# Broadcasting B by transposes of a repeated column in a Mamba kernel, with a new order of the front work

## The reference, cut to what matters

```
xi, z = split(x @ in_proj.T)
xc    = silu(causal_conv4(xi) + conv_b)
dt, B, C = split(xc @ x_proj.T)                    # 8, 16, 16 columns
delta = softplus(dt @ dt_w.T + dt_b)
h[t]  = exp(delta[t] * A) * h[t-1] + delta[t] * xc[t] * B[t]    # per channel and state
y[t]  = sum over the states of h[t] * C[t]
out_d = ((y + xc * D) * silu(z)) @ out_proj.T
```

## Time and profile before

| | us |
|---|---|
| median of 3 runs | 3480.59 |
| lowest, highest | 3477.56, 3481.06 |
| profiled execution | 3478.78 |
| its span, first to last instruction | 3477.0 |
| PE busy | 2952.8 (85%) |
| DVE busy | 3042.4 (88%) |
| ACT busy | 3106.2 (89%) |
| POOL busy | 2824.1 (81%) |
| mean granted clock of PE | 0.981 of 2.4 GHz |

### The profile page before, as it was taken

How to read it: one execution, slowest core, us unless ns; L and a number is a source line. 1 busy time by engine, 2 the same in 40 slices (tenths; PEclk the granted TensorE clock), 3 DMA queues, 4 the chain that set the end, 5 groups by cost and what they waited for, 6 DMA issues and landing times.

```text
span 3477.0 us, 53162 instructions
## 1 busy us (share of the span) xinstructions
PE 2952.8 (85%) x18432; PEld 2224.8 (64%) x18432; DVE 3042.4 (88%) x2456; ACT 3106.2 (89%) x5825; POOL 2824.1 (81%) x1701
## 2 busy tenths in 40 slices
PE   5888888888888888888888888888888888888885
PEld 3666666666666666666666666666666666666664
DVE  3889889889889888898898898899898988888986
ACT  4989999999989999999999998999999999999984
POOL 2788888888888888788788888888887888888886
PEclk9999999999999999999999999999999999999998
DMA  2222222222222222222222222222222222222221
GB/s 72 89 72 92 86 86 85 81 83 91 86 86 85 78 91 86 81 88 83 82 86 86 86 91 73 91 85 86 87 89 74 91 86 85 85 81 83 87 81 48
DMA packets 102319, 290.59 MB, mean 84 GB/s; under 512 B 11387, under 2 KB 36262, under 8 KB 102054
## 3 DMA queue, kind: packets, MB, share of 16 engines
q1 hardware_dynamic: 102054, 287.19, 25.4%
HBM read 276.91 MB, written 10.24 MB: 83 GB/s over the span
## 4 chain that ended last, share of the span: by engine, by line
ACT 33%; PE 31%; DVE 20%; issue 14%; POOL 1%; DVEq 0%; SPq 0%; DMA 0%; ACTq 0%; POOLq 0%
ACT da L697 13%; DVE hc L941 10%; PE g_ps L329 8%; DVE g_ps L928 8%; ACT w L643 7%; PE y_ps L329 5%; ACT L684 5%; PE m_ps L362 3%; PE m_ps L413 3%; PE m_ps L371 3%; PE m_ps L329 3%; PE m_ps L429 2%; PE m_ps L391 2%; DVE stats L914 2%; ACT s L667 1%
## 5 line engine op out<-in xcount | busy, mean ns | idle before, releaser
L834 POOL TENSOR_TENSOR hc<-hc,c_all 128x1000 f32<-128x1000 f32 x1024 | 2350.3, 2313 | 522.3 <-DVE hc L941 508.4
L941 DVE TENSOR_TENSOR_SCAN hc<-da,g_ps 128x1012 f32<-128x1012 f32 x1024 | 2274.6, 2253 | 91.4 <-ACT da L697 18.9
L697 ACT ACTIVATE da<-delta,a_neg 128x498 f32<-128x498 f32 x2048 | 1332.9, 700 | 9.0 <-DVE hc L941 7.3
L329 PEld LDWEIGHTS y_ps<-ident,hc 128*125 128x125 f32 x8192 | 1027.7, 190 | 238.8 <-issue 164.3
L329 PE MATMUL y_ps<-ident,hc 128*125 128x128 f32 x8192 | 1081.7, 275 | 2.2 <-POOL hc L834 2.2
L643 ACT ACTIVATE w<-ut,bt 125x256 f32<-125x256 f32 x2048 | 892.8, 497 | 2.9 <-ACT ut L630 0.4
L329 PE MATMUL g_ps<-ident,w 125*128 125x125 f32 x4096 | 547.3, 277 | 370.7 <-DVE hc L941 280.5
L329 PEld LDWEIGHTS g_ps<-ident,w 125*128 125x128 f32 x4096 | 443.9, 142 | 427.1 <-DVE hc L941 326.1
L928 DVE TENSOR_TENSOR g_ps<-u,g_ps 128x1000 f32<-128x1000 f32 x512 | 608.2, 1188 | 80.6 <-PE g_ps L455 80.3
L362 PE MATMUL m_ps<-zt,convw 128*128 128x500 f32 x1024 | 475.6, 587 | 0.7 <-ACT zt L573 0.7
L362 PEld LDWEIGHTS m_ps<-zt,convw 128*128 128x128 f32 x1024 | 190.5, 191 | 148.7 <-issue 121.9
(11 more groups left out here) (62 smaller groups left out, 2314.5 us busy)
## 6 DMA issues: line engine op xcount, KB each, us to landing
c_all<-c_rows SPq DMA_DIRECT2D x512, 500.0 KB, 3.6
xin<-x_t SPq DMA_DIRECT2D x32, 375.0 KB, 3.5
out<-out_sb SPq DMA_DIRECT2D x32, 250.0 KB
c_rows<-dbl SPq DMA_DIRECT2D x64, 31.2 KB, 1.6
c_all<-f_conv_w SPq DMA_DIRECT2D x1, 512.0 KB
c_all<-b_conv_w SPq DMA_DIRECT2D x1, 512.0 KB
hc<-f_in_w SPq DMA_DIRECT2D x1, 128.0 KB
inw<-f_in_w SPq DMA_DIRECT2D x1, 128.0 KB
```

What stands on the lines that cost most here:

```text
L329: return pe.matmul(dst, src, ident[0:rows, 0:rows], start=first, stop=last, is_transpose=True, skip_group_check=True)
L697: op = act.activation(states(da[n % RING])[j].rearrange("p (s t) -> p s t", s=SC)[:, :, 1:T], steps, ACT.Exp, scale=a_neg[:, p % 2, db, 2 ...
L834: pool.tensor_tensor(hc, hc, c_all[:, pair % CRING], ALU.mult).then_inc(hc_ready, 1)
L941: dve.tensor_tensor_scan(h[n % HRING][:, 0:UC], da[n % RING][:], g_ps[n % 2][:, 0:UC], 0.0, ALU.mult, ALU.add).then_inc(scanned, 1)
```

## The change

- B is taken to all partitions by transposes: for r in 0, 1, 3, 5 `fill_g` transposes `bt`'s column for the state, repeated 128 times as the stationary operand, in eight pieces of 125 tokens, in place of two bf16 matmuls. `parts`, `pick`, `minus`, the `split` jobs and copies, and the two inputs for them are gone.
- The front's order is x projection (5), dt (7), softplus (8), `bt` (8), y (9 and 10), u (10 and 11), transposed u (12 and 13). `turn` and the first half of the tail (`out_proj`, ACT's copy) go to step 13; the second half stays at 14. The gated products stand two units behind their y: before units 11 and 12.
- ACT's products for r = 6 and 7 are spread anew.
- `make_w` of POOL is rewritten too, but `W_POOL` is empty, so it isn't called.

```diff
-CONV, GATES, XPROJ, BT, SPLIT1, Y0, SPLIT2, Y1, DT, U0, U1, UT0, UT1 = 0, 4, 5, 6, 6, 6, 7, 8, 9, 11, 12, 13, 14
-TURN, TAIL0, TAIL1, TOKENS = 10, 11, 14, 15
+CONV, GATES, XPROJ, DT, SOFTPLUS, BT, Y0, Y1, U0, U1, UT0, UT1 = 0, 4, 5, 7, 8, 8, 9, 10, 10, 11, 12, 13
+TURN, TAIL0, TAIL1, TOKENS = 13, 13, 14, 15
...
-W_ACT = {2: [(-2, 4), (-1, 4)], 4: [(0, 2), (1, 2), (2, 2), (3, 2)], 6: [(6, 3), (7, 3), (8, 2)], 7: [(10, 2), (11, 3), (12, 3)]}
+W_ACT = {2: [(-2, 4), (-1, 4)], 4: [(0, 2), (1, 2), (2, 2), (3, 2)], 6: [(6, 3), (7, 3), (9, 2)], 7: [(9, 2), (10, 2), (11, 2), (12, 2)]}
...
-    ends = [("y", m - 2, 0), ("y", m - 2, 1), ("dt", m, 0)] if m > 1 else [("dt", m, 0)]
-    return ([("conv", m, 0), ("conv", m, 1), ("gate", m, 0), ("gate", m, 1), ("xproj", m, 0), ("bt", m, 0),
-             ("split", m, 1), ends[0], ("split", m, 2), *ends[1:], ("dt", m, 1)],
-            [("ut", m, 0), ("ut", m, 1)])
+    ends = [("y", m - 2, 0), ("y", m - 2, 1)] if m > 1 else []
+    return ([("conv", m, 0), ("conv", m, 1), ("gate", m, 0), ("gate", m, 1), ("xproj", m, 0),
+             ("dt", m, 0), ("dt", m, 1), ("bt", m, 0)] + ends, [("ut", m, 0), ("ut", m, 1)])
...
-                    src = w[w_index(p, r) % WRING]
-                    for e in range(2):
-                        for j in range(NT):
-                            at = e * BANK + j * TP
-                            mm = turned(g[:, at:at + TP], src[:, e, j, db * 128:(db + 1) * 128], TP)
-                    mm.then_inc(b_filled, 1)
-                else:
-                    if k <= 1:
-                        wait_drained(pe, "split", p, 2)
-                    pe.matmul(g[:, 0:TC], pick[:, 2 * r, :], parts[p % 2][:], start=True, stop=True)
-                    pe.matmul(g[:, BANK:UC], pick[:, 2 * r + 1, :], parts[p % 2][:],
-                              start=True, stop=True).then_inc(b_filled, 1)
+                elif k <= 1:
+                    wait_drained(pe, "bt", p, 0)
+                for e in range(2):
+                    for j in range(NT):
+                        if r in TURNED:
+                            rows = w[w_index(p, r) % WRING][:, e, j, db * 128:(db + 1) * 128]
+                        else:
+                            rows = bt[p % 2][:, j, 2 * r + e:2 * r + e + 1].broadcast_to([TP, 128])
+                        at = e * BANK + j * TP
+                        mm = turned(g[:, at:at + TP], rows, TP)
+                mm.then_inc(b_filled, 1)
...
                 m = bank("xproj", p, 0)
-                act.activation(dbl[:], m[0:XR, 0:TC], ACT.Copy)
-                act.activation(parts[p % 2][:], m[0:K2, 0:TC],
-                               ACT.Copy).then_inc(drained[bank_of("xproj", p, 0)], 1)
+                act.activation(dbl[:], m[0:XR, 0:TC], ACT.Copy).then_inc(drained[bank_of("xproj", p, 0)], 1)
...
-                        if k == DT:
+                        if k == SOFTPLUS:
                             load_set(SOFTPLUS_SET)
                             softplus(m + 1, 0)
                             softplus(m + 1, 1)
                             load_set(EXP_SET)
+                        if k == BT:
+                            bt_copy(m + 1)
...
-                    if m > 0 and k in (Y0 + 1, Y1 + 1):
-                        gated(m - 1, 0 if k == Y0 + 1 else 1)
+                    if m > 0 and k in (Y0 + 2, Y1 + 2):
+                        gated(m - 1, 0 if k == Y0 + 2 else 1)
```

More of the change, by code:

```diff
@@ L112, in all_jobs @@
         early, ends = front_jobs(m + 1) if m + 1 < PHASES else ([("y", m - 1, 0), ("y", m - 1, 1)], [])
-        jobs += early
+        jobs += early + ends
         jobs += [("turn", i + 1, 0)] if d == 0 and i + 1 < NCH else []
-        jobs += [("tail", i - 1, 0)] if d == 0 and i > 0 else []
-        jobs += ends
-        jobs += [("tail", i - 1, 1)] if d == 0 and i > 0 else []
+        jobs += [("tail", i - 1, 0), ("tail", i - 1, 1)] if d == 0 and i > 0 else []
         jobs += [("tokens", i + 2, 0)] if d == 1 and i + 2 < NCH else []
@@ L380, in xproj @@
                 mm.then_inc(job_filled, 1)
[L382 to L386, removed]
             def dt_proj(p, db):
@@ L479, in _ @@
             xproj(0)
+            dt_proj(0, 0)
+            dt_proj(0, 1)
             turn_b(0)
[L481 to L484, removed]
             turn_u(0, 0)
@@ L504, in _ @@
                             xproj(m + 1)
+                        if k == DT:
+                            dt_proj(m + 1, 0)
+                            dt_proj(m + 1, 1)
                         if k == BT:
                             turn_b(m + 1)
-                        if k == SPLIT1:
-                            split(m + 1, 1)
                     if m > 0 and k == Y0:
                         y_back(m - 1, 0)
-                    if m == 0 and k == Y0:
-                        dt_proj(1, 0)
-                    if front and k == SPLIT2:
-                        split(m + 1, 2)
                     if m > 0 and k == Y1:
                         y_back(m - 1, 1)
-                    if front and k == DT:
-                        if m > 0:
-                            dt_proj(m + 1, 0)
-                        dt_proj(m + 1, 1)
-                    if more and k == TURN:
-                        turn(i + 1)
-                    if d == 0 and i > 0 and k == TAIL0:
-                        out_proj(i - 1, 0)
                     if front:
@@ L529, in _ @@
                             turn_u(m + 1, 1)
+                    if more and k == TURN:
+                        turn(i + 1)
+                    if d == 0 and i > 0 and k == TAIL0:
+                        out_proj(i - 1, 0)
                     if d == 0 and i > 0 and k == TAIL1:
@@ L619, in bt_copy @@
             def bt_copy(p):
-                if p > 1 and W_POOL:
-                    act.wait_ge(w_pool, len(W_POOL) * (p - 1))
+                if p > 1:
+                    act.wait_ge(b_filled, UNITS * (p - 1))
+                    if W_POOL:
+                        act.wait_ge(w_pool, len(W_POOL) * (p - 1))
                 m = bank("bt", p, 0)
@@ L708, in _ @@
             xproj(0)
-            bt_copy(0)
-            split(0, 1)
             load_set(SOFTPLUS_SET)
             softplus(0, 0)
-            split(0, 2)
             softplus(0, 1)
@@ L717, in _ @@
                 decay(n)
+            bt_copy(0)
             ut_copy(0, 0)
@@ L762, in _ @@
                             ut_copy(m + 1, 1)
+                    if more and k == TURN:
+                        zt_copy(i + 1)
+                    if d == 0 and i > 0 and k == TAIL0:
+                        out_half(i - 1, 0)
                     if d == 0 and i > 0 and k == TAIL1:
```

34 lines of the change are left out of this document (5 added, 29 removed).

## The result

| | before | after |
|---|---|---|
| median us | 3477.56 (3476.34 to 3481.06) | 3496.40 (3494.44 to 3500.31) |
| span of the profiled execution | 3477.0 | 3492.4 |
| PE busy | 2952.8 | 3151.1 |
| ACT busy | 3106.2 | 3021.6 |
| DVE busy | 3042.4 | 3038.7 |

Both kernels were measured again side by side, five runs each, so the median before differs a little from the one above. The changed kernel is slower: ratio 1.0053, 95% interval 1.0038 to 1.0068. The forecast was 3444 us, a gain. The sign of the change is wrong, although the time lies inside the stated range of 3370 to 3545.

What follows compares the result with a forecast made beforehand. It took DVE's work plus its stalls as the bound. Even phases +0.5 us, odd −1.55, so −1.1 per pair times 32 = −35, lead-in −2: 3478.8 to 3442, 3444 us on the median's scale; range 3370 to 3545.

Steps and rivals of the forecast that it cites:

- unit 6, even and odd: DVE's stall before unit 6, whose slower fill brings data at T+8.1 (T: start of unit 4's fill): 0.45 us per phase.
- unit 10 without the clock: DVE's stall for unit 10's fill, which stands behind `bt` and the first softplus: 1.2 us in even phases, 1.5 in odd.
- unit 10, half clock: Odd phases: PE's work after idling 2.9 us before `bt` may run at half clock; half of 1.34 us added, 0.7.
- units 15 and 0: End of even phases: `turn`, `out_proj` and u transposes in units 12 to 14 stall DVE 1.8 and 1.25 us, together 3.05.
- kernel before: DVE's stalls in the unchanged kernel: 4.24 us per even phase and 4.2 per odd one.
- The gated product without a wait: DVE's 205.2 us of waits before the gated product go to nothing, since y is ready before units 11 and 12.
- the new fill's pitch: Eight transposes of a repeated column on PE take 0.91 us per fill, against 0.42 for the two bf16 matmuls.
- the lead-in: The serial start of the kernel loses three copies of 0.57 us: −2 us.
- PE bound by the fill: Rival: fills from a repeated column take longer than 0.94 us, making PE the bound; 3508 to 3604 us, middle 3550; 17%.
- The half clock in every phase: Rival: PE's idle before `bt` brings half clock everywhere, +0.65 us in odd and +1.35 in even phases; about 3508 us; 7%.
- The clock falls because of the transposes: Rival: transposes don't hold PE's full clock, so fills and sums run at half clock; +526 us, 3970 us; 3%.
- The waits vanish altogether: Rival: ACT reaches the first softplus before PE reaches `bt`, so stalls of 1.2, 1.5 and 0.7 us go; 3335 us; 12%.

## Why the prediction was wrong

| per pair, us | forecast | after, measured |
|---|---|---|
| unit 6, even and odd | 0.45 + 0.45 | 0.85 + 0.35 |
| unit 10 without the clock | 1.2 + 1.5 | 1.61 + 1.98 |
| unit 10, half clock | 0.7 | 1.6 |
| units 15 and 0 | 1.8 + 1.25 | 2.20 + 1.19 |
| sum | 7.35 | 9.8 |
| kernel before | 8.44 | 8.7 |

The steps that failed are sizes: the half clock behind the wait before `bt`, and the stall of unit 10 at full clock. The waits' total of 307.1 us gives 9.6 per pair where the sum here is 9.8, as the first and the last pair lack some of the stalls.

- **The gated product without a wait, the new fill's pitch, the place of every new stall: right.** 0.6 us at line 910, 0.86 against 0.91, and all six stalls of DVE are the six that were named. PE's waits before `bt` were forecast at 1.45 and 2.9 us and are 1.58 and 3.12. So the mechanism stood. The forecast was −1.1 per pair, a difference of 7.35 and 8.44, and sizes that were nearly all a little low turned it into +0.9 (9.6 against 8.7). That the time lies inside the range says little for the forecast: the range was wide enough for both signs.
- **The half clock: the term most under-sized**, by 0.9 per pair, 30 us. I took half of 1.34 us and gave odd phases alone a chance of it. In the trace 22 of the 30 odd phases with the long wait had it, and 13 of the 32 even ones (stalls of 2.0 to 3.2 for 1.61). In an odd one it costs up to 2.16 us (4.14 against 1.98 of stall): sum, fill and skip matmuls all stand between the wait and unit 10, not one pair of matmuls as in the earlier trace rows. Keeping PE busy in the wait settles it at 53 us, 1.65 per pair.
- **Unit 10 without the clock: 0.9 short, 28 us.** 0.14 per phase of it, 9 us, is a slip of addition: T+8.1 plus two units of 3.49 and two of 2.19 is T+19.46, not 19.6, and so in odd phases. The rest is a late softplus. In the even phase shown, T is 1554.43. The replay had the softplus end at T+18.25; it ended at T+18.9, `bt`'s transposes started at T+19.0, and the data of unit 10 were there at T+21.6 instead of 20.8. ACT was late ahead of the gates already: its table load for the convolution outputs stood at T+2.2 before (1769.40) and at T+2.8 now (1557.21), behind a wait for PE's sum:

```profile
1554.60 0.60 ACT L618 ACTIVATE yts<-y_ps 125x512 f32<-125x512 f32 x1 [0.82 <-PE y_ps L317]
```

  Such waits of ACT are 83.6 us in all where they were 13.0, since PE has next to no spare in the convolution units. That this makes the softplus late I read from the timeline; no run tested it.
- **Unit 6: 0.3 short, 10 us.** In the even phase the gates also waited 0.24 us for ACT. The run with the tail's second half at step 15 shows how a delay of PE at unit 0 is carried on: 0.35 became 1.20 in the odd phase.
- **The tail: 0.34 short, 11 us.** Unit 15 stalls 2.20, for 1.8.
- **The kernel before: its stalls were 8.7 and not 8.44**, 9 us the other way, and the lead-in gave 3.8 of wait for 2.

Terms: 30 + 28 + 10 + 11 − 9 = 70, less 7 for what the first and last pair lack, on the forecast's −35: +28 us in stalls, and 28 were measured in the waits. The lead-in has 3.8 less and all other idle time of DVE some 5 less, so its idle time grows by 19.1 us; its busy time falls by 3.7, and that leaves the 15.4 between the spans.

Of the rivals, *PE bound by the fill* needed a pitch above 0.94; it was 0.86. *The half clock in every phase* named a right cause of the slower side. Its 3508 us is close to what came partly by luck: it priced the clock at 86 us in all, the 22 of the forecast included, where 53 were measured, and the other low terms made up for that. It spoke against the even phases from waits of 1.67 and 1.54 us that stood at full clock; behind waits of 1.58 us the half clock came in 13 of 32. It had 7%, too little, as the one example before the change already had a wait of 1.90 us and a clock of 0.55 behind it. *The clock falls because of the transposes* is refuted: between 1529.8 and 1541.5 us PE ran 91 matmuls, all of them transposes, at 1.00, and at 1628.2 the clock is 0.50 behind a wait. The Trainium skill ("TensorE: Matmul & The Clock Gate", Part 4, PE-mode transpose) has it that the full clock isn't engaged by transpose mode; this trace, whose fills and sums use that mode, doesn't agree. *The waits vanish altogether* was priced at 3335 us for the end of the softplus wait. That wait alone was worth 36 us, because the products for unit 14 came right behind it: the price left out what is late next. With the softplus wait, the products and the tail all moved the kernel takes 3302.

## What to carry to other kernels

When four engines are each near 90% and serve one another in order, replay the edit up to the point where the next wait begins, and price each stall with what stands right behind it; two waits in series hide each other, so test them removed together before either is called worthless. A forecast made as a small difference of large stalls is uncertain in its sign. In this kernel already an idle time of PE of 1.6 us could bring the half clock, so such a wait needs a price for it over all that stands between it and the next one who waits. Where a small job shares a bank in turn with a slow producer's output (`bt` with the softplus), put it ahead: here that took away waits of 145.7 us, though the time only followed once the next wait was gone too.

## What the runs showed of the hardware

- Waits of PE of 1.58 to 3.13 us were followed by a stretch at the lower level (0.50 of 2.4 GHz) in some phases and not in others with the same wait: behind 3.12 us at 1523 the clock stayed at 1.00, behind 3.13 at 1628 it was 0.50; behind 1.58 us at 1573 the work ran at full pace, behind 1.58 at 1145 the clock was 0.64. It was seen in other kernels behind waits of 1.95 us (8 transposes in 1.69 for 1.04 us, clock 0.55), 2.01 (`out_proj` 3.32 for 1.9, clock 0.57) and 2.05 us (gates 3.58 for 1.86, clock 0.58). Matmuls of zeros in the wait brought the clock back, and 53 us with it.
- A stationary operand read from one repeated column costs what an ordinary one costs: 279 against 273 ns for the transpose, 142 against 141 ns for the load, over 4096 of each in the changed kernel.
